# A graph network on one core: self weights copied by ScalarE, and a second stage that tests and tells by eight pairs

## The reference

```
z  = (1 + eps) * x + segment_sum(x[src], dst)
z  = relu(z @ W1 + b1) @ W2 + b2
z  = batchnorm over the nodes(z) * gamma + beta + x
x1 = layernorm(x + z)
v  = relu(segment_sum(edge_weight * x1[src], dst) @ W3)
y  = layernorm(x1 + v)
```

## Time and profile before

| | us |
|---|---|
| median of 3 runs (4477.64 to 4486.39) | 4478.68 |
| the profiled execution's own time | 4476.26 |
| its span, first to last instruction | 4473.0 |
| POOL busy | 3318.0 |
| PE busy | 3437.8 |
| DVE busy | 2623.7 |
| ACT busy | 414.0 |

### The profile page before, as it was taken

The page is one execution under the profiler, slowest core; times in us unless marked ns, Lnnn a source line. Parts: engine busy times, 40 slices in busy tenths (PEclk is TensorE's granted clock), DMA queues, the critical chain, the costliest instruction groups (busy, mean ns, idle before and its releaser), DMA issues.

```text
span 4473.0 us, 69589 instructions
## 1 busy us (share of the span) xinstructions
PE 3437.8 (77%) x16131; PEld 2829.6 (63%) x16132; DVE 2623.7 (59%) x5747; ACT 414.0 (9%) x1055; POOL 3318.0 (74%) x3456
## 2 busy tenths in 40 slices
PE   2787877877777777787654888888888888888887
PEld 2676766666666666666543666666666666666665
DVE  3888877776787777687656334344434444443443
ACT  0000000000000000000044000000000000000001
POOL 6777777777777777777734777777777777777775
PEclk7888988988988898888866999999999999999999
DMA  5343333433343333333386334434443444334343
GB/s 144 107 114 111 112 112 110 116 112 109 113 115 113 110 112 114 111 111 112 106 266 202 113 113 120 119 115 118 120 119 115 119 120 119 115 119 119 115 119 101
DMA packets 305380, 540.19 MB, mean 121 GB/s; under 512 B 85290, under 2 KB 197790, under 8 KB 305326
## 3 DMA queue, kind: packets, MB, share of 16 engines
q0 software_dynamic: 159424, 434.52, 33.5%
q10 hardware_dynamic: 89348, 67.77, 5.0%
q1 hardware_dynamic: 56554, 37.24, 2.8%
HBM read 489.80 MB, written 46.88 MB: 120 GB/s over the span
## 4 chain that ended last, share of the span: by engine, by line
POOL 62%; issue 22%; PE 5%; DVE 5%; DMA 3%; POOLq 1%; DVEq 1%; ACT 1%; ACTq 0%; SPq 0%; PEldq 0%
POOL ring L619 31%; POOL ring L553 30%; PE ps L1284 2%; PE ps L1494 1%; DMA x_dram<-ring 1%; DMA ring<-x_dram,idx 1%; DVE work L889 1%; POOLq L630 1%; PE ps L1367 1%; DVEq L380 1%; DMA z_dram<-z_pair 1%; DVE work L886 0%; ACT ring L1725 0%; DMA ring<-in_x,idx 0%; POOL ring L566 0%
## 5 line engine op out<-in xcount | busy, mean ns | idle before, releaser
L553 POOL DMA_INDIRECT ring<-in_x,idx x1664 | 1708.6, 1027 | 502.8 <-issue 473.1
L619 POOL DMA_INDIRECT ring<-x_dram,idx x1612 | 1524.0, 945 | 517.7 <-issue 489.8
L1494 PE MATMUL ps<-ring,work 128*128 x6448 | 1521.4, 391 | 339.8 <-SPq L529 337.8
L1494 PEld LDWEIGHTS ps<-ring,work 128*128 128x128 f32 x6448 | 1217.6, 193 | 629.4 <-issue 472.1
L1155 DVE TENSOR_SCALAR work<-ps,dstT,wT 128x256 f32<-128x256 f32 x1612 | 742.2, 539 | 1129.9 <-PE ps L1494 1057.9
L1284 PE MATMUL ps<-ring,ones_sb 128*128 x3324 | 935.8, 431 | 390.2 <-SPq L459 348.5
L1284 PEld LDWEIGHTS ps<-ring,ones_sb 128*128 128x128 f32 x3324 | 694.7, 216 | 549.2 <-issue 443.4
L901 DVE SCALAR_TENSOR_TENSOR ones_sb<-dstT,tile_base,minus_iota 128x256 f32<-128x256 f32 (+1 forms) x294 | 318.5, 1110 | 226.5 <-issue 187.3
L1367 PEld LDWEIGHTS ps<-work 128*128 128x128 f32 x3384 | 429.8, 197 | 17.9 <-DVE work L889 2.9
L1367 PE MATMUL ps<-work 128*128 128x128 f32 x3384 | 428.3, 279 | 2.1 <-DVE work L889 2.1
L886 DVE TENSOR_TENSOR work<-ps,current 128x768 f32<-128x768 f32 x282 | 267.8, 950 | 9.1 <-PE ps L1367 9.1
(11 more groups left out here) (245 smaller groups left out, 2178.6 us busy)
## 6 DMA issues: line engine op xcount, KB each, us to landing
ring<-in_x,idx POOLq DMA_INDIRECT x1664
ring<-x_dram,idx POOLq DMA_INDIRECT x1612, 2.7
z_dram<-z_pair ACTq DMA_DIRECT2D x49, 256.0 KB, 3.2
ones_sb<-x_dram ACTq DMA_DIRECT2D x49, 256.0 KB
ring<-z_dram SPq DMA_DIRECT2D x24, 512.0 KB, 6.0
ring<-in_x SPq DMA_DIRECT2D x24, 512.0 KB, 7.3
x_dram<-ring ACTq DMA_DIRECT2D x24, 512.0 KB, 3.8
out<-ones_sb ACTq DMA_DIRECT2D x48, 256.0 KB
```

The lines of the kernel that those rows point to most:

```text
L553: nc.gpsimd.indirect_dma_start(out=ring[:, q, c, :], out_offset=None, in_=x, in_offset=bass.IndirectOffsetOnAxis(ap=idx[:, q, c:c + 1], ax ...
L619: nc.gpsimd.indirect_dma_start(out=ring[:, q, c, :], out_offset=None, in_=x1_dram, in_offset=bass.IndirectOffsetOnAxis(ap=idx[:, q, c:c + ...
L1494: last = nc.tensor.matmul(to[:, t * D:(t + 1) * D], ones_of[:, b, c, t * P:(t + 1) * P], ring[:, ds((p + b) & (RING - 1), 1), c, :].rearra ...
```

## The change

- POOL no longer copies self weights, and `self_next` and its loads are gone. ACT copies them, eight pairs at a time, from `selfT` into the ring (`selves`), and counts `s_selfed`. It does so for tiles 0 and 1 ahead of the first block, for tile 2k+2 behind the sum of tile 2k, and for tile 2k+3 at the end of block k.
- ACT waits for that until PE has entered the old pairs. `s_entered` starts at 32.
- SP tells of landed gathers without a wait for self weights; PE waits for `s_selfed` itself, once per tile.
- The tile's table has two more numbers, `FROM` and `UPTO`: which eight-pair blocks ACT copies for a tile. DVE computes them with six more operations, and drops the copy of 32 rows of `selfT` behind its end.
- Second stage: POOL tests the list's end at every eight pairs, and waits at every four; SP waits for eight pairs and tells of eight.

```diff
 SP, first stage
                         for g in range(4):
                             sp.wait_ge(s_gathered[g], r * (32 * QUARTER) + 32 * QUARTER)
-                            stand(sp)
-                            sp.wait_ge(s_selfed, r * 4 + g + 1)
                             sp.sem_inc(s_landed, QUARTER)
...
-                                sp.dma_start(self_next[:, h * HALF:(h + 1) * HALF, :],
-                                             selfT[:, ds((i + 1) * RING + h * HALF, HALF), :]).then_inc(s_idx[h], 16)
 SP, second stage
-                for g in range(RING // TWO):
-                    with sp.If(r * RING + g * TWO < pairs2):
-                        sp.wait_ge(s_row2[g], r * (32 * TWO) + 32 * TWO)
-                        sp.sem_inc(s_landed2, TWO)
+                for g in range(4):
+                    with sp.If(r * RING + g * QUARTER < pairs2):
+                        sp.wait_ge(s_row2[g], r * (32 * QUARTER) + 32 * QUARTER)
+                        sp.sem_inc(s_landed2, QUARTER)
 POOL, first stage
-            pool.wait_ge(s_selves, 1)
-            for q in range(0, RING, QUARTER):
-                selves_of(q, selfT)
             pool.wait_ge(s_table, 1)
...
-                            pool.wait_ge(s_entered, r * RING + (q - RING + FOUR + 1))
+                            pool.wait_ge(s_entered, r * RING + (q + FOUR + 1))
...
-                        if (q + 1) % QUARTER == 0:
-                            selves_of(q + 1 - QUARTER, self_next)
 POOL, second stage
-                    for q in range(h * HALF, (h + 1) * HALF, TWO):
+                    for q in range(h * HALF, (h + 1) * HALF, QUARTER):
...
                         with pool.If(r * RING + q < pairs2):
-                            pool.wait_ge(s_added2, r * RING + q + 2)
-                            stand(pool)
-                            for b in range(TWO):
-                                for c in range(2):
-                                    gather2(q + b, c)
+                            for f in range(q, q + QUARTER, FOUR):
+                                pool.wait_ge(s_added2, r * RING + f + FOUR)
+                                stand(pool)
+                                for b in range(FOUR):
+                                    for c in range(2):
+                                        gather2(f + b, c)
 PE, in sum_tile
                 pe.wait_ge(s_onehot, head + counted + TILE_ONES)
+                stand(pe)
+                pe.wait_ge(s_selfed, upto + sweep * 4)
+                stand(pe)
                 pe.wait_ge(s_landed, low + first)
...
+            pe.sem_inc(s_entered, RING)
 ACT
+            def selves(j):
+                *_, sweep, begin, upto = entry(act, j)
+                with act.If(begin < upto):
+                    with act.Fori(begin, upto) as b:
+                        act.wait_ge(s_entered, b * QUARTER + sweep * RING + (QUARTER + 1))
+                        stand(act)
+                        nc.scalar.activation(ring_self[:, ds((b & 3) * QUARTER, QUARTER), :], selfT[...], ACT.Copy).then_inc(s_selfed, 1)
...
                 summed(k, 0)
                 if loads:
+                    selves(2 * k + 2)
                     load_x(k + 1)
...
                 if old >= 3:
                     keep_z(k - 3)
+                if loads:
+                    selves(2 * k + 3)
...
             act.wait_ge(s_selves, 1)
+            selves(0)
+            selves(1)
```

More of the change, by code:

```diff
@@ L180, in gnn @@
         unsorted_p = sb("unsorted_p", [P, 1], f32)
-        row = work[0:1, 4000:4000 + 12 * (NT + 1)].rearrange("p (a t) -> p a t", a=12)
-        row_i = work[0:1, 5200:5200 + 3 * NT].bitcast(i32).rearrange("p (a t) -> p a t", a=3)
+        row = work[0:1, 4000:4000 + 14 * (NT + 1)].rearrange("p (a t) -> p a t", a=14)
+        row_i = work[0:1, 5400:5400 + 5 * NT].bitcast(i32).rearrange("p (a t) -> p a t", a=5)
         flag = sb("flag", [1, 3], f32)
-        table = sb("table", [1, NT, 10], mybir.dt.uint16)
+        table = sb("table", [1, NT, 12], mybir.dt.uint16)
         sweeps = sb("sweeps", [1, 1], i32)
@@ L354, in gnn @@
         s_idx2 = [sem(f"s_idx2_{h}") for h in range(2)]
-        s_row2 = [sem(f"s_row2_{g}") for g in range(RING // TWO)]
+        s_row2 = [sem(f"s_row2_{g}") for g in range(4)]
         s_landed2 = sem("s_landed2")
@@ L401, in stand @@
             eng.sem_inc(s_passed[eng.engine], 1)
-        NEW, HEAD, M4, M2, END, LOW, REP, SHARED, OFF, SWEEP = range(10)
+        NEW, HEAD, M4, M2, END, LOW, REP, SHARED, OFF, SWEEP, FROM, UPTO = range(12)
         NEW2, M42, HEAD2, M22, END2, PREV2 = range(6)
@@ L620, in gather2 @@
                     out=ring[:, q, c, :], out_offset=None, in_=x1_dram,
-                    in_offset=bass.IndirectOffsetOnAxis(ap=idx[:, q, c:c + 1], axis=0)).then_inc(s_row2[q // TWO], 16)
+                    in_offset=bass.IndirectOffsetOnAxis(ap=idx[:, q, c:c + 1], axis=0)).then_inc(s_row2[q // QUARTER], 16)
             with pool.Fori(0, rounds2) as r:
@@ L731, in _ @@
             sync()
+            from_i, upto_i = row_i[:, 3, :], row_i[:, 4, :]
+            setup(nc.vector.scalar_tensor_tensor(out=from_i, in0=newly, scalar=float(QUARTER - 1), in1=tmp, op0=ALU.add, op1=ALU.subtract))
+            setup(nc.vector.scalar_tensor_tensor(out=upto_i, in0=new, scalar=float(QUARTER - 1), in1=tmp, op0=ALU.add, op1=ALU.subtract))
+            sync()
+            setup(nc.vector.tensor_scalar(from_i, from_i, 3, None, ALU.arith_shift_right))
+            setup(nc.vector.tensor_scalar(upto_i, upto_i, 3, None, ALU.arith_shift_right))
+            sync()
+            setup(nc.vector.tensor_copy(table[0:1, :, FROM], from_i))
+            setup(nc.vector.tensor_copy(table[0:1, :, UPTO], upto_i))
             for column, of in ((NEW, newly), (HEAD, end), (M4, send), (M2, begins), (END, new), (LOW, slo)):
@@ L893, in ones_of_tile @@
             def ones_of_tile(j, bank):
-                new, head, m4, m2, _, _, _, shared, off, sweep = entry(dve, j)
+                new, head, m4, m2, _, _, _, shared, off, sweep, _, _ = entry(dve, j)
                 counted = sweep * RING + off
@@ L1270, in sum_tile @@
             def sum_tile(j, bank, others):
-                new, head, m4, m2, end, low, rep, _, off, sweep = entry(pe, j)
+                new, head, m4, m2, end, low, rep, _, off, sweep, _, upto = entry(pe, j)
                 first = sweep * RING
```

24 lines of the change are left out of this document (12 added, 12 removed).

## The result

| | us |
|---|---|
| kernel before, median of 4 runs beside it (4477.64 to 4488.28) | 4482.53 |
| changed kernel, median of 4 runs (4513.32 to 4516.53) | 4514.89 |
| ratio, with its 95% interval | 1.0071 [1.0057, 1.0085] |
| the profiled execution's own time, before and after | 4476.26, 4516.53 |

The change makes the kernel slower by 32 us where 15 were forecast; 4514.9 lies just above the range's end of 4514.

What follows compares the result with a forecast made beforehand. POOL's gathers, one per 1.25 us, were taken as the bound. Start -8.1, copies -4.0, loop +11.9 and tail +15.4 gave +15.2 us on 4478.68: 4493.9 us, range 4465 to 4514 for 8 in 10 runs.

Steps and rivals of the forecast that it cites:

- part 3: First stage's loop: DVE's table read, 0.44 us longer per tile, makes each turn 0.44 longer in 27 blocks: +11.9 us.
- Rival A: First stage: the loop doesn't hold POOL, its copies are worth 10 us, gaps stay: -2.7 us, 4476; chance 0.24.
- part 2: POOL's copies between gathers: 0.10 us each, none won in the loop, only in the other 20 blocks: -4.0 us.
- Part 1: Start: PE begins earlier, so POOL needn't wait for it and gather 65 starts at 93.6: 8.1 us won.
- S: Rival from the experiments, not the prediction: ScalarE's copies and table reads delay PE; 4515 us for Experiment 1; no chance given.
- E: Rival: ScalarE's copies come late and hold PE; from 10 us up, 4505; chance 0.03.
- Part 4: Second stage's loop: gathers keep 1.25 us, PE's bursts cause no wait, testing by eights adds four gathers: +5.0 us.
- The tail: Kernel's end: PE's last step starts 14.4 us later, plus 1.0 for the lower clock: +15.4 us, bounds 12.4 and 19.
- The 136 us: First stage: time by which gathers exceed 945 ns, laid to DVE's one-hot writing, 98 times, 1.39 us each.
- B: Rival, first stage: one-hot gaps come out short, a block loses 0.4 us less: -22.7 us, 4456; chance 0.12.
- C: Rival, first stage: a turn's first gap falls just under 0.62, losing 2.1 instead of 0.94: 32 more, 4526; chance 0.09.
- D: Rival, second stage: PE can't keep up in bursts, POOL waits up to 1 us per eight: up to 4590; chance 0.04.

Runs made afterwards that it cites:

- Experiment 1: The changed kernel with DVE reading only the first 10 of a table row's 12 numbers: 4487.78 us, ratio 1.0011 to the kernel before.
- Experiment 3: DVE's one-hot writing reads one operand from PSUM: in the kernel before 4382.78 us, ratio 0.9759; in the changed kernel 4403.69 us, ratio 0.9823.

## Why the prediction was wrong

**The step that failed: part 3, the loop.** It said that "the first L901 of a turn is 0.44 later, so in the loop a turn is 42.65 + 0.44 us" and that "the first keeps 0.94 to 1.05". A turn has two tiles and two table reads, and I counted one. Each read lengthens its own way: from the first to the second group DVE takes 832.82 - 814.62 = 18.20 us instead of 17.82, and from the second to the next first one 858.00 - 832.82 = 25.18 instead of 24.83. POOL restarts at the end of each group, so it forgets one gap before it comes to the next. Both gaps move, the first as well: 0.64 + 0.44 = 1.08, or more where the copy's 0.10 stood in its way. The losses of a turn grow by 0.9 to 1.1 us, two copies give back 0.2, and the turn is 0.7 to 0.9 us longer instead of 0.44: some 22 us over 27 blocks, where 11.9 were put down. From gather 65 to gather 1664 the two profiles differ by 24.0 us, where 7.9 were forecast. Experiment 1 shows it: with 10 numbers the first gap is 0.66 again. What was said of the second (1.68, a loss of 1.95) came out to 0.01 us.

**Rival A's 10 us for the copies** can't be had beside it: some 8 of them come back as time between gathers and are lost again as gap, as part 2 had it. The other blocks didn't win the 4 us put down for them. Under the one-hots the 27 blocks of the loop lose 24 us more than before and the 20 others 11 more; why in those was not tested. These 20 also lost 2.8 us each before, not the 3.3 that the prediction read.

**Part 1, the start,** was mis-sized: 3.4 us for 8.1. The wait went as said, but the tiles that PE could now begin early bring their own one-hots under the first 64 gathers, whose last one starts 4.7 us later. A stall that goes lets in what stood behind it, here onto the same engine.

**Parts 3 and the rivals S and E, ScalarE:** right at 0. PE waited for its copies three times, 14.5 us in all, and POOL, a ring ahead, didn't notice.

**Part 4** was right: 1616 gathers of 945 ns, 1.25 us apart, +4.9 for 5.0, and no wait for PE to speak of once they have begun (2.4 us, in pieces of at most 0.3).

**The tail** was right in its mechanism and 2.5 us short: the landing of the last gather is told 5.2 us after its start, not 3.9; the first step lost 2.2 us of clock, not 1.0; the steps between followed 1.2 us closer than forecast; and behind the last step 1.2 us were put at nothing. Together with part 4 it is 17.8 us of the profile and 19.2 measured alone.

**The 136 us.** The prediction set the rows above the inference of the Trainium skill, "SBUF — State Buffer", section "Who interferes with whom", that two SBUF inputs don't hurt descriptor generation. Experiment 3 decides for the rows: with one input in PSUM, 1708.6 - 1589.4 = 119 of the 136 us are gone, and the instructions of L901 take 1101 ns instead of 1110.

**Range and chances.** The forecast case came nearest, but the time lies outside its own 4480 to 4510, which was drawn round +15 with an error in a term of 12 us. Of the rivals none came as it was put. A: the gaps didn't stay. B and C: they grew, away from the edge. D: its premise came in part, the second stage's mean granted clock falls from 0.98 to 0.92, but POOL didn't wait. E: POOL didn't wait for ScalarE's copies.

## What to carry to other kernels

Where a periodic engine is held up by another one's instruction, the cost is a function of the gap between their starts. Work out the gap of every meeting in a turn, each from the interval between two meetings modulo the period, before trusting that "later" costs only what it is late; here two entries more in a table that DVE reads cost 27 us at POOL. Better is to remove the meeting, though the price then moves: with the gathers free, the same two entries cost 0.43 us a tile on DVE, which bounds the stage (experiment 3). Here one operand moved to another memory gave 2.4% on chips like the first. And telling by larger groups costs at the end of a list, where every step behind the last landing counts in full.

## What the runs showed of the hardware

- A SCALAR_TENSOR_TENSOR on DVE with both inputs in SBUF (three of them, 3.3 us) holds back the indirect DMAs that POOL issues, by 0.94 to 2.1 us; with one input in PSUM it doesn't (1027 and 955 ns a gather in the mean).
- A read of a table row into registers costs by the number: on DVE 6 in 1.39 us, 10 in 2.27, 12 in 2.71; on PE 10 in 2.39 and 12 in 2.86, on ScalarE 12 in 2.57.
- Chips differ. On the slower kind a gather still takes 945 ns and the second stage's 1612 take 2388 to 2412 us instead of 2014 to 2018, since POOL waits between them; PE's mean granted clock is 0.82 instead of 0.90, and PE stops between matmuls (248 us at L1367 against 2.0). DVE idles 1554 us before L1155 instead of 1135. The changes above weigh differently: 0.976 on one kind and 1.022 on the other for the same edit.
- Behind 3.75 us of idleness 16 matmuls took 5.82 us at a mean granted clock of 0.62, instead of 3.62 at 1.00.
